# Six of twelve weight conversions on GpSimd instead of ScalarE, with new opening lists for all engines: cross attention and a ternary FFN on one core

## The reference

```python
def _weight_quant(w):
    scale = 1.0 / jnp.clip(jnp.mean(jnp.abs(w)), 1e-05)
    wq = jnp.clip(jnp.round(w * scale), -1.0, 1.0) / scale
def _act_quant(x):
    scale = 127.0 / jnp.clip(jnp.max(jnp.abs(x), axis=-1, keepdims=True), 1e-05)
    xq = jnp.clip(jnp.round(x * scale), -128.0, 127.0) / scale
...
x = x + _L0_xattn_ref(_layernorm(x), ctx_768, Wq, Wk, Wv, Wo, bo)   # 8 heads of 64
h = silu(bitlinear(ln, w_gate)) * bitlinear(ln, w_up)               # inner width 2048
x = x + bitlinear(h, w_down)                                         # ln = _layernorm(x)
```

## Time and profile before

| quantity | value |
|---|---|
| median of three runs | 1103.38 us (1101.78 to 1104.1) |
| span of the profiled execution | 1103.9 us |
| PE busy | 1079.8 us (98%) |
| DVE busy | 965.3 us (87%) |
| ACT busy | 742.6 us (67%) |
| POOL busy | 501.5 us (45%) |

### The profile page before, as it was taken

The page is one execution under the profiler, slowest core; times in us unless marked ns, Lnnn a source line. Parts: engine busy times, 40 slices in busy tenths (PEclk is TensorE's granted clock), DMA queues, the critical chain, the costliest instruction groups (busy, mean ns, idle before and its releaser), DMA issues.

```text
span 1103.9 us, 17477 instructions
## 1 busy us (share of the span) xinstructions
PE 1079.8 (98%) x5528; PEld 496.4 (45%) x5528; DVE 965.3 (87%) x2081; ACT 742.6 (67%) x947; POOL 501.5 (45%) x645
## 2 busy tenths in 40 slices
PE   8879999999999999999999999999999999999998
PEld 6434444444444444444444444444444444444443
DVE  5997898998889988888989988888899889988985
ACT  3997767757656667777665677777666656666543
POOL 0255554565445454554444446555543444344111
PEclk9998999999999999999999999999999999999999
DMA  9997665353555635544564553655455555554334
GB/s 352 281 241 149 117 125 114 82 116 87 110 124 122 123 86 106 118 88 106 121 123 91 109 115 91 106 116 114 98 105 119 119 107 104 106 110 96 72 77 100
DMA packets 355963, 133.80 MB, mean 121 GB/s; under 512 B 332448, under 2 KB 332960, under 8 KB 355360
## 3 DMA queue, kind: packets, MB, share of 16 engines
q1 hardware_dynamic: 355872, 132.70, 54.4%
HBM read 34.08 MB, written 16.78 MB: 46 GB/s over the span
## 4 chain that ended last, share of the span: by engine, by line
PE 78%; DVE 7%; ACT 2%; issue 1%; DMA 1%; POOL 0%; SPq 0%; DVEq 0%; ACTq 0%; POOLq 0%
PE ps L1401 35%; PE ps L1422 18%; PE ps L1337 8%; PE ps L1340 8%; PE ps L1338 8%; DVE FF L1074 1%; DVE hm L1083 1%; PE ps L1330 1%; DVE hm L1078 1%; PE ps L1325 1%; DMA FF<-FF 1%; DVE bns L1060 1%; ACT FF L851 0%; DVE am L1128 0%; DVE xr L1066 0%
## 5 line engine op out<-in xcount | busy, mean ns | idle before, releaser
L1401 PE MATMUL ps<-wgT,FF 128*128 128x512 bf16 x1024 | 263.1, 379 | 1.6 <-ACT FF L851 1.6
L1401 PE MATMUL ps<-wW,FF 128*128 128x512 bf16 x1024 | 262.8, 379 | 0.3 <-DVE FF L1074 0.3
L1422 PE MATMUL ps<-wW,FF 128*128 128x512 bf16 x1024 | 231.5, 379 | 1.1 <-DVE xr L1066 0.9
L851 ACT ACTIVATE FF<-ps,sgu 128x512 f32<-128x512 f32 x256 | 173.1, 680 | 62.7 <-PE ps L1401 60.8
L1074 DVE TENSOR_TENSOR FF<-FF,ps 128x512 f32<-128x512 f32 x256 | 173.8, 681 | 47.2 <-ACT FF L851 26.7
L860 ACT ACTIVATE FF<-FF,c 128x1024 int16<-128x1024 f32 x128 | 141.1, 1141 | 73.8 <-DVE c L1087 73.6
L706 POOL TENSOR_TENSOR AT<-AT,rd 128x512 f32<-128x512 f32 x64 | 67.7, 1057 | 220.1 <-DVE rd L1119 216.5
L1422 PEld LDWEIGHTS ps<-wW,FF 128*128 128x128 bf16 x1024 | 99.8, 98 | 122.6 <-issue 2.1
L1401 PEld LDWEIGHTS ps<-wW,FF 128*128 128x128 bf16 x1024 | 99.7, 98 | 122.5 <-DVE FF L1074 3.8
L1401 PEld LDWEIGHTS ps<-wgT,FF 128*128 128x128 bf16 x1024 | 97.7, 98 | 123.9 <-issue 4.5
L694 POOL TENSOR_TENSOR xhl<-xn,xhl 128x512 f16<-128x512 f32 x64 | 74.3, 1161 | 85.1 <-ACT xhl L867 85.1
(11 more groups left out here) (146 smaller groups left out, 1751.9 us busy)
## 6 DMA issues: line engine op xcount, KB each, us to landing
xr<-in_x SPq DMA_DIRECT2D x64, 256.0 KB, 2.8
out<-xr SPq DMA_DIRECT2D x64, 256.0 KB, 2.3
FF<-in_L_ffn_w_gate SPq DMA_DIRECT2D x4, 1024.0 KB, 12.3
wW<-in_L_ffn_w_up SPq DMA_DIRECT2D x4, 1024.0 KB, 15.4
FF<-in_L_ffn_w_down SPq DMA_DIRECT2D x4, 1024.0 KB, 6.3
FF<-FF SPq DMA_TRANSPOSE x192, 3.3
MV<-in_L_xattn_Wq SPq DMA_DIRECT2D x1, 1024.0 KB, 8.4
MV<-in_L_xattn_Wo SPq DMA_DIRECT2D x1, 1024.0 KB, 15.7
```

The costliest lines, as they stand in the source:

```text
L851: eng.activation(h[:, i % 2, f * 512:(f + 1) * 512], G[n % 2][:, :], ACT.Silu, scale=sgu[:, 0, i % W:i % W + 1]).then_inc(a_si, 1)
L1401: mm = eng.matmul(bank[n % 2][:, :].rearrange("p (o f) -> p o f", o=4), qxT[:, i % 2, k, :], w[:, 4 * f:4 * f + 4, k, :], start=(k == 0), ...
L1422: mm = eng.matmul(y_bank(i)[:, :], hT[:, i % 2, c, :], wdT[:, c, :], start=(c == 0), stop=(c == 15))
```

## The change

`tern 0 1`, `tern 0 3`, `tern 1 0`, `tern 1 2`, `tern 2 0` and `tern 2 2` are issued on GpSimd as a `tensor_scalar` multiplication from float32 to int16, and count a semaphore of their own, g_wq. `clip` of these waits for g_wq, and of the other six for a_wq with a smaller count. The five lists of `OPENING` are replaced by others; the pieces in them are the same but for the six that move, and the due times behind the lists are unchanged. In the changed kernel lines are shifted (by 8 to 12 on ACT, DVE and PE, by -2 on SP and most of POOL).

```diff
+        g_wq = sem("g_wq")
...
+        TERN_G = ((0, 1), (0, 3), (1, 0), (1, 2), (2, 0), (2, 2))
...
             "sync": (
-                "load_ctx, load_x 2, load_wk, load_wq, load_gate 0, load_wv, load_gate 3, load_x 0, load_gate 1, "
...
+                "load_x 1, load_x 0, load_ctx, load_x 2, load_wk, load_wq, load_x 3, load_gate 0, load_gate 2, "
+                "load_gate 1, turn_x 0, load_wv, load_bo, load_gate 3, load_up 0, turn_x 1, load_up 2, load_up 1, "
...
             "gpsimd": (
-                "constants, rstd 0 0, x_lo 0, rstd 1 0, x_lo 1, add_bo 0, rstd 2 0, p_norm 0, x_lo 2, rstd 3 0, "
...
+                "constants, rstd 0 0, rstd 1 0, x_lo 0, add_bo 0, x_lo 1, add_bo 1, rstd 2 0, tern 0 1, rstd 3 0, "
+                "tern 0 3, add_bo 2, rstd 4 0, x_lo 2, tern 1 0, tern 1 2, p_norm 0, p_lo 0, x_lo 3, p_norm 1, rstd 5 "
...
@@ block.gpsimd
+            def tern(m, c):
+                n = TURNED.index((m, c))
+                eng.wait_ge(v_wc, m + 1)
+                eng.wait_ge(l_w[m][c], 16)
+                if n >= 2:
+                    eng.wait_ge(v_wn, n - 1)
+                eng.tensor_scalar(tern_dst(m, c), raws[m][:, c, :], wst[:, m, 2:3], None, ALU.mult).then_inc(g_wq, 1)
+
+            for m, c in TERN_G:
+                put(TERN_T[m][c], tern, m, c)
...
@@ block.scalar
             for m, c in TURNED:
-                put(TERN_T[m][c], tern, m, c)
+                if (m, c) not in TERN_G:
+                    put(TERN_T[m][c], tern, m, c)
...
@@ block.vector
             def clip(m, c):
                 n = TURNED.index((m, c))
-                eng.wait_ge(a_wq, n + 1)
+                if (m, c) in TERN_G:
+                    eng.wait_ge(g_wq, TERN_G.index((m, c)) + 1)
+                else:
+                    eng.wait_ge(a_wq, n + 1 - sum(TURNED.index(mc) < n for mc in TERN_G))
```

More of the change, by code:

```diff
@@ L398, in xattn_ffn @@
             "sync": (
-                "load_ctx, load_x 2, load_wk, load_wq, load_gate 0, load_wv, load_gate 3, load_x 0, load_gate 1, "
-                "load_x 1, load_gate 2, load_up 0, load_up 1, load_wo, load_bo, load_up 3, load_x 3, load_up 2, "
[17 rows of a table removed]
-            "gpsimd": (
[18 rows of a table removed]
-            "scalar": (
[30 rows of a table removed]
-            "vector": (
[38 rows of a table removed]
-            "tensor": (
[21 rows of a table removed]
+                "load_x 1, load_x 0, load_ctx, load_x 2, load_wk, load_wq, load_x 3, load_gate 0, load_gate 2, "
+                "load_gate 1, turn_x 0, load_wv, load_bo, load_gate 3, load_up 0, turn_x 1, load_up 2, load_up 1, "
[16 rows of a table added]
+            "gpsimd": (
[18 rows of a table added]
+            "scalar": (
[28 rows of a table added]
+            "vector": (
[37 rows of a table added]
+            "tensor": (
[21 rows of a table added]
         }
```

## The result

| | before | after |
|---|---|---|
| median, us | 1102.63 | 1121.11 (1118.74 to 1123.61, 4 runs) |
| ratio to before, 95% interval | 1 | 1.0167 [1.0145, 1.0189] |
| profiled span, us | 1103.9 | 1119.5 |
| predicted, us | | 1098.9 (1094.0 to 1104.5) |

The prediction was wrong in sign, and the time lies far outside its range. The kernel before has one more run here than ahead of the prediction (1101.88 us). A time is 1.8 us longer than the span of the same execution (1121.24 and 1119.5 us for the profiled one of the changed kernel), so the span of 1103.9 us is not a time of 1103.9, as the text ahead of the prediction has it, but belongs to an execution of some 1105.7 us, an estimate.

What follows compares the result with a forecast made beforehand. PE was taken as the bound from 131.3 us on, so only the opening could give time. 5.3 + 1.2 - 1.5 - 0.5 = 4.5 us off gave 1098.9 us; forecast range 1096 to 1101, wider range 1094 to 1104.5.

Steps and rivals of the forecast that it cites:

- The conversion's price: Each 2048-column conversion on POOL: 2.1 us, taken from a cast's row; 4.6 us kept as the upper end.
- my third rival: POOL conversions at 4.6 us each hold DVE: 1106.4 us, deciding from about 3.4 us; chance 0.15 shared with order trouble.
- The stall term: DVE held while POOL converts: half a conversion, 1.0 us, each; 2.5 us up to `mean 2`, 1.5 for the last two.
- POOL's queue: Behind the FFN's start, `tern 2 2` waits for `clip 2 0` with other POOL pieces queued behind it: 0.5 us lost.
- ACT's relief and DVE's early start: Opening up to `gate_up 0 0`: `total 2` at about 77.7 and first FFN matmul near 92, worth 5.3 us.
- nothing would change behind 135 us: Stage behind 135 us: unchanged with PE 99.7% busy; at most 2.6 us of idle to win from 131 to 350 us.
- SP's queue: DMA queue with `turn_x 0` and `turn_x 1` ahead of loads: costed at nothing, a microsecond or two if 3 us later.
- scores 7: PE's 2.19 us wait at 131.26 for a transposing DMA, `turn_x 7` now ahead of `turn_h 0`: 1.2 us gained.

Runs made afterwards that it cites:

- late5: The changed kernel with each of POOL's six conversions as 5 instructions of 256 columns, 768 of 2048 columns left at zero: 1113.45 us, 1.0092.
- short128: The changed kernel with each POOL conversion on the first 128 of 2048 columns, the others left at zero: 1105.93 us, 1.0020.
- short1024: The changed kernel with each POOL conversion on the first 1024 of 2048 columns, the others left at zero: 1106.64 us, 1.0037.
- order_only: The changed kernel's new lists with all twelve conversions on ACT: 1108.42 us, 1.0047.
- my one test of it: New lists, all conversions on ACT, with the first two transposes of the DMA queue moved behind the loads: 1123.68 us, 1.0190.
- turn7: The kernel before with `turn_x 7` ahead of `turn_h 0 1` on the DMA queue: 1103.58 us, 0.9995.
- hold4: New lists, all conversions on ACT, plus a full-size unread POOL conversion at the first four of the six places: 1117.73 us, 1.0124.
- lock_only: New lists, all conversions on ACT, plus a full-size unread POOL conversion at each of the six places: 1126.52 us, 1.0207.
- pieces8: The changed kernel with each whole POOL conversion cut into 8 pieces of 256 columns: 1128.73 us, 1.0221.

## Why the prediction was wrong

*The conversion's price* failed first and worst. I took 2.1 us, with 4.6 as the upper bound; it is 5.45, above both and above the 3.4 at which my third rival was to decide. The step was "the cast has one input as the conversion has": I matched the number of inputs and not the operation.

*The stall term* failed in size and in form. I charged 1.0 us for each conversion, 4 us in all; the hold costs 8 us (`late5` against after). The mechanism was right and so was the sign of the rival that rested on it, but the rival stopped at 1106.4. Most of the miss is the length again: between 30 and 125 us DVE's stretched forms (`den` scales, `clip`s, `max_fold` copies, `x_norm`s, two casts of 128x512) take some 23 us more in the changed kernel than in `short128`, 3.8 us for each conversion. That is 0.7 of a conversion where I had charged half. A 0.17 us scale that meets the start of a conversion loses nearly all of it.

*POOL's queue*, 0.5 us in my sum, and the late results with it are 6 to 8 us. At 2.1 us each they would have been about nothing (`short1024` against `short128`, 0.0017 with overlapping intervals).

*ACT's relief and DVE's early start*, 5.3 us at the first FFN matmul, is what short conversions test. `short128` has that matmul at 94.32, a gain of 2.2 us, and still ends at 1.0020 [1.0003, 1.0036].

```profile
94.32 1.04 PE L1419 MATMUL ps<-wgT,FF 128*128 128x512 bf16 x4 [0.38 <-DMA FF<-FF]
```

As `order_only` has it at 96.47 with the same lists, the early start by itself brought nothing there and ACT's relief the 2.2 us. So two steps failed: the sum was more than twice too large, and it was not kept. I had said that nothing would change behind 135 us. The stage from 131.3 to 200 us in the kernel before and in `short128`:

```profile
131.30:200.00 68.70, 68.08 (x376) 31.02 (x377) 60.38 (x133) 49.79 (x65) 36.33 (x46) 1.00 0.51 105
```
```profile
131.30:200.00 68.70, 64.93 (x340) 29.16 (x338) 64.55 (x141) 46.48 (x64) 30.91 (x43) 1.00 0.49 93
```

PE idles 3.8 us there instead of 0.6: the new lists give the gain back where I hadn't looked, waiting for DVE and ACT between the FFN's stages (1.92 us at 134.74 the longest).

*SP's queue* was costed at nothing, with two up quarters behind `turn_x 1` where the list has three; the "wait near 26 us" came at 28.84 behind a chain over POOL that I hadn't followed. Its price stays open, since my one test of it made a wait of its own. It is inside the 0.0020 to 0.0047 that the lists cost.

*`scores 7`*, 1.2 us: open. In the traces of `turn7` and before it is about 1 us; the times don't resolve it.

The account of the 0.0167: lists with short conversions 0.0020 to 0.0037, POOL's queue and late results 0.0055 to 0.0072, hold of DVE 0.0075, each give or take some 0.003. How the middle one divides into queue and late results is not settled: unread conversions cost less than real ones at four places (`hold4` 1.0124 against 1.0167) and more at six (`lock_only` 1.0207), but these kernels have all twelve conversions on ACT as well, and `lock_only` the wait of my making.

## What to carry to other kernels

Before work moves to POOL, time that very operation there: two operations of one input each differed by 2.9 times. Price the engine that it moves to by what stands behind it in the queue and by which DVE pieces can meet it, and cut a long one into pieces only if the queue can bear the extra length. When lists are written anew, follow the gain to the stage where the bound engine no longer waits, because time won before the FFN (`short128`) can be gone 40 us later, and half of a wait taken out (`turn7`) came back as another.

## What the runs showed of the hardware

- POOL: `tensor_scalar` from f32 takes 5.44 us for 128x2048 and 2.84 for 128x1024 to int16, bf16 or f32 alike where tried, by pointer or immediate; a cast or copy of 128x2048 takes 1.89. The Trainium skill's "GPSIMD Engine Reference", section "Elementwise — side-by-side cycle accounting", has about 2.6 cycles per element as the floor for two inputs, 1.03 where the ports bound the loop and about 1.8 for a tight loop. The one-input scale here is above all of these: 2.66 ns is some 3.2 cycles by that page's 1.2 GHz, an estimate. The measured time is thus also above the 1.8 to 3.1 us that the prediction had worked out from the page.
- DVE pieces held by POOL appear as busy time of their own, 5.03 us for a 128x8 scale, with no wait shown. The number of instructions in a window gives it away (72 instead of 86 with the same lists).
- A POOL `tensor_scalar` of 256 columns takes 0.92 us (median in `pieces8`, the longest 2.33), so a cut into 8 makes 5.45 us into 7.4 to 7.8, and once 9.7.
